# A graph layer on one core: moving the Q and V products of twelve node tiles out of the G stage, with x handed in transposed

## The chip, the cores and the metric

The kernel runs on one core of a Trainium2 chip. The metric is the device time of one execution in microseconds; lower is better. Three timed runs of the kernel before gave 1563.94, 1565.83 and 1568.54 us. The engines are called PE (TensorE, with PEld for its weight loads), DVE (VectorE), ACT (ScalarE), POOL (GpSimd) and SP (SyncE, here used only to start DMAs).

## The reference

One layer over N = 6250 nodes with D = 512 features and 106,250 directed edges (50,000 random ones in both directions, and one self loop per node), sorted by destination. All weights are 512 x 512.

```python
Q = relu(x @ Wq + bq);  V = x @ Wv + bv
# _former: attention without a softmax
Q = relu(layer_norm(Q));  H = sum(Q, axis=1)**2
H = pi / (2 * 2*(max(H) - min(H))) * H
cosQ, sinQ = Q * cos(H), Q * sin(H)
former = (cosQ @ (cosQ.T @ V) + sinQ @ (sinQ.T @ V)) / (cosQ @ sum(cosQ) + sinQ @ sum(sinQ) + 1e-10)
# _gcn: every node sums its neighbours' rows of G = x @ Wg
gcn = segment_sum((x @ Wg)[src] * dinv[src] * dinv[dst], dst) + bg     # dinv = 1/sqrt(degree)
out = relu(layer_norm(former + gcn + V) * gamma + beta)
return layer_norm(x + out)
```

## The kernel before

The nodes are cut into 49 tiles of 128 (the last has 106 rows); each matrix product with x is carried as three products of rounded parts (hi x hi, hi x lo, lo x hi), so one tile of x times one weight matrix is 12 matmuls of 128x512. There are two long parts.

**The G stage** (`g_tile`, tiles t = 0 to 48). SP loads a tile of x; PE turns it with four transposes (`g_turn`, L1363), ACT rounds the turned tile to its hi part (`g_step`, L601), DVE makes the lo part (`g_split`, L959), PE multiplies by Wg (12 matmuls, L1320 to L1322), ACT copies the result to SBUF (`g_keep`, L605). Beside it:
- For the first 31 tiles PE and DVE also count the node degrees: per tile three sets of one-hot rows (`bins`, L948 on DVE, 27 small matmuls L1376 on PE).
- ACT squares each tile of G (`square`, L610): 8 of them early, then from tile 31 on three per tile. From tile 35 on the gather table is written: ACT makes the hi half of a row pair (`pair_hi`, L616), DVE the lo half (`pair_split`, L865), SP stores it to DRAM (`table_store`, L403). Three or four pairs go with each tile (`pairs_until`), in a ring of 4 buffers: `pair_hi(n)` waits until pair n-4 has been stored. In five of these iterations DVE first works out scale factors (`factors`, L851 to L858) for the next group.
- For the first 37 tiles the hi and lo parts are stored to DRAM (`xt_store`), 512 KB a tile, to be loaded again later. For the last 12 tiles (`FUSED = 12`) PE makes Q and V at once from the parts that are there (`qv_beside_g`, 24 matmuls), and DVE and ACT carry them on.

Within one iteration of ACT the order is: round tile t+2, keep G of tile t, squares, `pair_hi`. Within one iteration of DVE it is: split tile t+2 (which waits for ACT's round), factors, then `pair_split` of the pairs that ACT made an iteration earlier. On SP it is: load of a coming tile, then the table stores.

**The run of 882 steps** (49 destination tiles with 18 steps each). Each step gathers the table rows of 128 edges: POOL issues an indirect DMA (L550), DVE makes a one-hot matrix (L1066), PE adds them up with two f16 matmuls (`chunk`, L1436 and L1438). The other work is laid between these chunks by tables of numbers: `qv_at(t)` starts Q and V of a tile every 6 steps (37 tiles, the first three before step 0), `cos_at` and `sin_at` run the two sweeps of moments (every 10/3 and every 3 steps a tile; 14 and 12 f16 matmuls each), `out_at` the output (every 7 steps a tile). Between the loops stand short serial parts (angles, moments). Every 18 steps the finished destination tile is combined with V and with the tile's own rows of G, which are loaded back from the table (`own_load`, `add_own`, two DVE instructions).

Of the kernel before, what the change touches and what calls it, by code (L numbers as in the profile page):

```python
# [6 lines left out]
F32 = mybir.dt.float32  # L7
# [31 lines left out]
def build_layer(nc, x, src, dst, Wq, bq, Wv, bv, Wg, bg, gamma, beta, out):  # L39
    N, D = x.shape  # L40
    E = src.shape[0]
# [16 lines left out]
    COLS = GROUPS * P  # L58
    LN_EPS = 1e-5
# [9 lines left out]
    COS_END = COS_AT + 10 * (TILES - 1) // 3 + 3  # L69
    SIN_AT = COS_END + 6  # L70
    SIN_END = SIN_AT + 3 * (TILES - 1) + 3
    OUT_AT = SIN_END + 6
    assert B == 4 and TAIL and FULL == 48 and SCALED < QV_TILES and OUT_AT + 7 * FULL < STEPS
# [7 lines left out]
    turned_x = nc.dram_tensor("turned_x", [TILES * P, 2 * D], F32).ap()  # L81

    ctx = ExitStack()
    with ctx:
# [16 lines left out]
        with nc.sbuf_tensor("operands_f16", [P, 8, 2 * D], F16) as operands_f16:  # L101
            pass
# [41 lines left out]
        edge_banks = banks[6], banks[7], banks[0], banks[6]  # L144
# [7 lines left out]
        dst_nat = part(0).bitcast(I32)  # L152
        src_nat = part(12).bitcast(I32)
        src_f = part(13)
# [20 lines left out]
        own_rows = pairs[:, 0, :]  # L175
# [48 lines left out]
        WIDE = 32  # L224

        def x_slot(t):
            return t % 2 if t < WIDE else t % 4

        def x_loads_until(t):
            return sum(x_slot(u) == x_slot(t) for u in range(t + 1))  # L230
# [5 lines left out]
        for name in (  # L236
            "setup_done", "pads_set", "dst_loaded", "src_loaded", "bias_loaded", "g_x_turned",
            "pair_hi", "pair_split", "factors_ready", "squared", "dst_placed", "own_added", "own_linked", "own_loaded", "combined_stored",
# [5 lines left out]
            "q_kept", "q_roomed", "q_hi", "q_paired", "late_roomed", "late_hi", "late_paired", "v_squared", "angle_ready", "cos_sin_ready", "m_summed", "m_hi", "moment_ready",  # L244
            "moment_hi", "sums_kept", "sums_turned", "cs_rounded", "o_products", "o_hi", "o_norm_ready", "o_stats1", "o_squared1", "o_squared2",
            "o_final", "o_scaled2", "dve_chain", "edges_f", "ident_ready", "raw_split",
            "edges_turned", "edges_kept", "limits_ready", "limits_turned", "ranges_ready",
# [10 lines left out]
        x_loaded = [sem(f"x_loaded{n}") for n in range(3)]  # L258
        xt_stored = [sem(f"xt_stored{n}") for n in range(4)]
# [28 lines left out]
        def nth(t):  # L288

            return (t + FUSED) % TILES  # L290

        def q_tile(t):

            return tile_of(nodes, nth(t))

        def qv_at(t):
            return 6 * (t - QV_RING)

        def cos_at(t):
            return COS_AT + 10 * t // 3  # L300

        def sin_at(t):
            return SIN_AT + 3 * t

        def out_at(n):
            return OUT_AT + 7 * n
# [5 lines left out]
        LAST_TILE = {4: 4, 7: 3, 9: 4, 10: 5, 12: 6, 13: 7, 15: 9, 16: 10, 17: 11}  # L312

        def late(t, at):

            return LAST_TILE[at] if t == QV_TILES - 1 else at

# [7 lines left out]
        def q_room(t):  # L325

            n = nth(t) % 2
            return stage[:, n, :] if t < QV_TILES else pairs[:, 1 + n, 0:D]

        def pair_at(n):  # L330

            return 8 + 12 * n

        def squares_room(t):
            return stage[:, 2, :] if t < QV_TILES else combine[:, 0:D]

        def v_slot(t):
            return t % QV_RING if t < QV_TILES else 1 + nth(t) % 2

        def v_stores_before(t):  # L340
            return t // QV_RING + (v_slot(t) > 0) * (FUSED // 2) if t < QV_TILES else nth(t) // 2

# [8 lines left out]
        def _(sp):  # L351

            whole, left = (GROUPS - 1) * P, E // P - (GROUPS - 1) * P

            def edge_views(nat):
                return nat.rearrange("p (g e) -> p g e", e=P)

            def full_groups(ap, nat, arrived):
                sp.dma_start(edge_views(nat)[:, 0:GROUPS - 1, :],
                             ap[0:whole * P].rearrange("(g p e) -> p g e", p=P, e=P)).then_inc(arrived, 16)  # L360

            def last_group(ap, nat, arrived):
                sp.dma_start(edge_views(nat)[0:left, GROUPS - 1, :],
                             ap[whole * P:(whole + left) * P].rearrange("(p e) -> p e", e=P)).then_inc(arrived, 16)
                sp.dma_start(edge_views(nat)[left:left + 1, GROUPS - 1, 0:E - E // P * P],
                             ap[E // P * P:E].rearrange("(p e) -> p e", p=1)).then_inc(arrived, 16)

            full_groups(dst, dst_nat, s["dst_loaded"])
            sp.wait_ge(s["pads_set"], 1)
            last_group(dst, dst_nat, s["dst_loaded"])  # L370
            def g_load(t):
                r, n = rows_of(t), x_slot(t)
                if t in (WIDE + 2, WIDE + 3):
                    sp.wait_ge(s["degrees_summed"], 1)
                else:
                    sp.wait_ge(s["g_x_turned"], freed(t, 2 if t < WIDE + 2 else 4))
# [33 lines left out]
            for t in range(0, TILES):  # L410
                if t <= WIDE:
                    g_load(t + 2)
# [1238 lines left out]
```

## Time and profile before

| | |
|---|---|
| runs | 1563.94, 1565.83, 1568.54 us; median 1565.83 |
| profiled execution, first to last instruction (span) | 1564.0 us |
| PE / PEld busy | 1493.1 us (95%) / 942.9 us (60%) |
| DVE / ACT / POOL busy | 1060.7 (68%) / 497.6 (32%) / 921.2 us (59%) |
| mean granted TensorE clock | 0.982 |
| G stage, up to the first chunk on PE | 313.7 us |
| from the first chunk to the end | 1250.3 us |

The span is the whole program on the device; what lies around it in a timed run is the 1.8 us to the median. A busy share is an average over stages, so the rows below go stage by stage. On PE a matmul is pipelined: the duration shown for a 128x512 matmul is 0.38 to 0.40 us, but the next one starts 0.21 to 0.24 us after it, and it is these distances between starts that add up to the time.

### The profile page before, as it was taken

What the parts mean: (1) busy time and instruction counts of PE and PEld (TensorE: products, weight loads), DVE (VectorE), ACT (ScalarE), POOL (GpSimd) and SP (SyncE); (2) the same over time, 40 slices, a digit from 0 to 9 for tenths busy, and PEclk for the clock granted to TensorE, in tenths of its full rate; (3) what the DMA queues carried; (4) which work ended last, traced back from release to release, by engine and by line L of the source; (5) the groups of instructions that cost most, each with busy time, mean ns of one, the idle gap of its engine ahead of it and who ended that gap; (6) DMA issues with size and microseconds to landing.
All of it is one profiled execution on the core that took longest, in us unless ns stands there. A gap on an engine that the chain in (4) does not pass through costs nothing.

```text
span 1564.0 us, 24480 instructions
## 1 busy us (share of the span) xinstructions
PE 1493.1 (95%) x7911; PEld 942.9 (60%) x7911; DVE 1060.7 (68%) x2945; ACT 497.6 (32%) x1010; POOL 921.2 (59%) x1022
## 2 busy tenths in 40 slices
PE   5999999899999997999998999989999999999995
PEld 3777788666666663444443444437777777767763
DVE  6999577677777676444445544457878877878785
ACT  2322776533333222111111111113333333333332
POOL 0000000277777775777776777777777777777772
PEclk9999999999999997999999999999999999999997
DMA  6555544699999998889888999889999999999894
GB/s 237 183 183 183 175 157 150 235 311 311 331 309 331 299 325 246 286 286 302 284 285 260 292 296 307 294 248 314 298 290 311 304 294 294 312 288 309 279 315 130
DMA packets 172753, 423.84 MB, mean 271 GB/s; under 512 B 24142, under 2 KB 25802, under 8 KB 172616
## 3 DMA queue, kind: packets, MB, share of 16 engines
q0 software_dynamic: 71120, 236.74, 48.1%
q1 hardware_dynamic: 79980, 146.16, 27.3%
q10 hardware_dynamic: 21516, 39.29, 6.6%
q8 instruction: 65, 1.06, 0.3%
q14 instruction: 72, 0.59, 0.1%
HBM read 351.42 MB, written 70.67 MB: 270 GB/s over the span
## 4 chain that ended last, share of the span: by engine, by line
PE 83%; DMA 6%; DVE 6%; issue 2%; ACT 2%; POOL 1%; SPq 0%; POOLq 0%; DVEq 0%; ACTq 0%
PE bank L1320 18%; PE bank L1321 17%; PE bank L1322 17%; PE bank L1436 12%; PE bank L1438 11%; DMA gathered<-scaled_g,index_slots 3%; DVE stage L948 2%; PE bank L1567 1%; PE bank L1376 1%; DMA stage<-in_x 1%; PE bank L1363 1%; POOL gathered L550 1%; DMA combine<-values 1%; PE bank L1504 1%; PE bank L1507 1%
## 5 line engine op out<-in xcount | busy, mean ns | idle before, releaser
L550 POOL DMA_INDIRECT gathered<-scaled_g,index_slots x882 | 882.9, 1001 | 305.7 <-issue 187.7
L1066 DVE TENSOR_SCALAR one_hot<-iota_bf,dst_in_tile,gathered 128x128 bf16<-128x128 bf16 x882 | 268.8, 326 | 327.4 <-DMA gathered<-scaled_g,index_slots 300.5
L1320 PE MATMUL bank<-weights,operands 128*128 128x512 f32 x784 | 395.5, 504 | 6.6 <-DVE stage L966 6.1
L1436 PE MATMUL bank<-gathered,one_hot 128*128 128x512 f16 x882 | 344.1, 390 | 25.7 <-DVE one_hot L1066 25.6
L1438 PE MATMUL bank<-gathered,one_hot 128*128 128x512 f16 x882 | 339.0, 384 | 0.0
L1321 PE MATMUL bank<-weights,operands 128*128 128x512 f32 x784 | 311.3, 397 | 0.0
L1322 PE MATMUL bank<-weights,operands 128*128 128x512 f32 x784 | 310.7, 396 | 0.0
L535 POOL COPY dst_slots<-dst_cols 128x18 f32 x49 | 13.9, 284 | 301.8 <-issue 299.6
L1320 PEld LDWEIGHTS bank<-weights,operands 128*128 128x128 f32 x784 | 149.1, 190 | 69.4 <-DVE stage L966 7.0
L1436 PEld LDWEIGHTS bank<-gathered,one_hot 128*128 128x128 bf16 x882 | 85.9, 97 | 171.1 <-issue 74.9
L707 ACT ACTIVATE operands_f<-operands,cos_sin_v 128x512 f16<-128x512 f32 x98 | 69.5, 720 | 335.8 <-PE bank L1322 201.6
L1322 PEld LDWEIGHTS bank<-weights,operands 128*128 128x128 f32 x784 | 148.1, 189 | 36.3
L1321 PEld LDWEIGHTS bank<-weights,operands 128*128 128x128 f32 x784 | 149.3, 190 | 22.6
L1322 PE MATMUL bank<-operands_f,nodes 128*128 128x512 f16 x392 | 148.5, 379 | 0.0
L1320 PE MATMUL bank<-operands_f,nodes 128*128 128x512 f16 x392 | 148.5, 379 | 0.0
L1321 PE MATMUL bank<-operands_f,nodes 128*128 128x512 f16 x392 | 148.5, 379 | 0.0
L724 ACT ACTIVATE operands<-stage,stats 128x512 fp32r<-128x512 f32 x98 | 70.9, 724 | 218.8 <-DVE stats L1203 218.8
L1438 PEld LDWEIGHTS bank<-gathered,one_hot 128*128 128x128 bf16 x882 | 87.9, 100 | 48.3 <-issue 3.6
L948 DVE TENSOR_TENSOR stage<-iota_bf,pairs 128x450 bf16<-128x450 bf16 (+1 forms) x186 | 95.6, 569 | 2.8 <-PE bank L1376 0.7
L1320 PE MATMUL bank<-gathered,operands 128*128 128x512 f32 (+1 forms) x196 | 84.8, 433 | 0.0
L1321 PE MATMUL bank<-gathered,operands 128*128 128x512 f32 (+1 forms) x196 | 78.5, 401 | 0.0
L1322 PE MATMUL bank<-gathered,operands 128*128 128x512 f32 (+1 forms) x196 | 78.2, 399 | 0.0
(231 smaller groups left out, 1916.3 us busy)
## 6 DMA issues: line engine op xcount, KB each, us to landing
operands<-values SPq DMA_DIRECT2D x98, 256.0 KB, 5.7
stage<-in_x SPq DMA_DIRECT2D x96, 256.0 KB, 3.8
turned_x<-operands SPq DMA_DIRECT2D x37, 512.0 KB, 3.1
operands<-turned_x SPq DMA_DIRECT2D x37, 512.0 KB, 6.4
gathered<-scaled_g,index_slots POOLq DMA_INDIRECT x882, 5.2
scaled_g<-pairs SPq DMA_DIRECT2D x49, 260.0 KB, 2.1
pairs<-scaled_g SPq DMA_DIRECT2D x49, 260.0 KB
values<-stage ACTq DMA_DIRECT2D x49, 256.0 KB, 4.8
```

What stands on the lines that cost most here:

```text
L550: pool.indirect_dma_start(out=plain(row_ring[k % RING]), out_offset=None, in_=table, in_offset=bass.IndirectOffsetOnAxis(ap=index_slots[:, ...
L707: act.activation(v_hi, m_values(g), ACT.Copy, scale=column(cos_sin_v, g % TILES * 2 + g // TILES))\
L724: act.activation(operands[:, 5 + n % 2, :], stage[:, 2 + j, :], ACT.Square, bias=st[:, 1:2], accum_out=st[:, 2:3]).then_inc(s[f"o_squared{ ...
L948: last = dve.tensor_tensor(hot[:, 0:count, :].rearrange("p c (j two) -> p c j two", two=2), iota_bf[:, 0:width].rearrange("p (j two) -> p ...
L1066: dve.tensor_scalar(one_hot[:, k % HOT, :], iota_bf[:, :], column(dst_in_tile, seq % 2 * PER_TILE + k), scale_of(row), ALU.is_equal, ALU.m ...
L1320: pe.matmul(out_ap, a_hi, b_hi, start=start and n == 0, stop=False, skip_group_check=True)
L1321: pe.matmul(out_ap, a_hi, b_lo, start=False, stop=False, skip_group_check=True)
L1322: last = pe.matmul(out_ap, a_lo, b_hi, start=False, stop=stop and n == len(pairs) - 1, skip_group_check=True)
L1363: last = pe.transpose(bank_[:, b * P:b * P + r], x_in[0:r, b * P:(b + 1) * P], ident[0:r, 0:r])
L1376: last = pe.matmul(banks[5][:, 0:TILES], mod_hot[half][:, c, :], div_hot[half][:, c, 0:TILES], start=False, stop=False, skip_group_check=True)
L1436: pe.matmul(gcn_banks[seq % 2][:, :], one_hot[:, k % HOT, :], hi, start=k == 0, stop=False, skip_group_check=True)
L1438: pe.matmul(gcn_banks[seq % 2][:, :], one_hot[:, k % HOT, :], lo, start=False, stop=False, skip_group_check=True).then_inc(s["chunk_summed ...
```

## The change

1. x is also handed in transposed by tiles and padded to 49 full tiles (`x_turned`), and the edge lists are handed in padded and in the layouts that the kernel used to make by transposing on PE. The transposes, `xt_store` and the loads of 512 KB go. ACT rounds and DVE splits straight from the loaded tile (`g_round`, `g_split`).
2. `FUSED` goes. The G stage makes G alone. All 49 tiles of Q and V are made in the run of steps; there x is loaded again (256 KB a tile) and split again by ACT and DVE (`x_round`, `x_split`).
3. The tables of numbers change: a tile of Q and V every 16/3 steps, of the sweeps every 20/7, of the output every 27/4. The number of steps stays at 882.
4. The own rows of G are added when V is made (`own_sum`, one DVE instruction, and a second store of 256 KB on ACT's queue), in place of `own_load` and `add_own`. The squares of V move from DVE to ACT (`v_square`).

The rules that pace the squares, the table's pairs and the factors (`squares_until`, `pairs_until`, `FACTOR_GROUPS`, `PAIRS = 4`) are the same.

```diff
-    FUSED = 12
-    QV_TILES = TILES - FUSED
-    HEAD, DRAIN = 6 * QV_RING, 24
-    LAST_QV = 6 * (QV_TILES - 1 - QV_RING)
+    HEAD, DRAIN = 18, 24
+    def qv_at(t):
+        return 16 * (t - QV_RING) // 3
+    LAST_QV = qv_at(TILES - 1)
     ANGLES = LAST_QV + 9
     COS_AT = ANGLES + 7
-            return COS_AT + 10 * t // 3
+        return COS_AT + 20 * t // 7
-            return SIN_AT + 3 * t
+        return SIN_AT + 20 * t // 7
-            return OUT_AT + 7 * n
+        return OUT_AT + 27 * n // 4
...
+            def g_load(t):
+                sp.wait_ge(s["g_summed"], freed(t, XT_RING))
+                sp.dma_start(operands_raw[:, 4 + t % XT_RING, :], x_turned[t, :, :])...
-            def xt_store(t): ...
+            def x_load(t):
+                if t < XT_RING:
+                    sp.wait_ge(s["g_summed"], done(TILES - XT_RING + t))
+                else:
+                    sp.wait_ge(s["q_summed"], freed(t, XT_RING))
+                sp.dma_start(operands_raw[:, 4 + qv_slot(t), :], x_turned[t, :, :])...
...
             for n in range(pairs_until(TILES - 1), TILES):
                 pair_hi(n)
-            for u in (TILES, TILES + 1, TILES + 2):
-                beside_g(u)
+            x_round(0)
...
+            x_split(0)
             for n in range(pairs_until(TILES - 1), TILES):
                 pair_split(n)
-            keep_beside_g(TILES)
...
+            def own_sum(t):
+                dve.scalar_tensor_tensor(own_room(t), q_tile(t), column(own_scale, t), v_room(t), ALU.mult, ALU.add)
-            def add_own(seq): ...
...
             def g_tile(t, n, r):
                 pe.wait_ge(s["g_x_split"], done(t))
-                if t + 2 < TILES:
-                    g_turn(t + 2)
                 pe.wait_ge(s["g_kept"], freed(t, 2))
                 ...
-                if t >= QV_TILES:
-                    qv_beside_g(t)
```

On ACT, in the last third of the G stage, an iteration stood like this before (round, keep, squares, pairs, then Q and V of an earlier tile):

```order
L601 CAST operands<-bank 128x512
L605 COPY nodes<-bank 128x512
L610 ACTIVATE squares_out,row_square<-nodes 128x512 x3
L616 ACTIVATE pairs<-nodes,row_factor 128x512 x3
L622 DMA values<-stage 128x512
L627 ACTIVATE nodes<-nodes 128x512
L632 ACTIVATE stats<-stats,small 128x1
L639 ACTIVATE nodes,row_sum<-nodes,stats 128x512
```

and stands like this now (`operands_raw` is the loaded tile of transposed x):

```order
L530 CAST operands<-operands_raw 128x512
L538 COPY nodes<-bank 128x512
L543 ACTIVATE squares_out,row_square<-nodes 128x512 x3
L549 ACTIVATE pairs<-nodes,row_factor 128x512 x3
L530 CAST operands<-operands_raw 128x512
```

The four rows of Q and V are gone; round, keep, three squares and the pairs are as they were.

On DVE, at the very end of the G stage, a last set of factors was followed by the last table pairs and then V, Q and the square of V of the last fused tile. Now the split of the first x tile for the steps (L877) stands between the factors and the last four pairs:

```order
L773 TENSOR_TENSOR row_factor<-row_factor,dinv 128x4
L877 TENSOR_TENSOR operands<-operands_raw,operands 128x512
L780 SCALAR_TENSOR_TENSOR pairs<-nodes,row_factor,pairs 128x512
L781 COPY pairs<-row_scale 128x1
L780 SCALAR_TENSOR_TENSOR pairs<-nodes,row_factor,pairs 128x512
L781 COPY pairs<-row_scale 128x1
```

So the last pairs wait behind an instruction that waits for ACT to have made all pairs' hi halves and rounded that tile.

On DVE, between the chunks of the Q and V loop, this piece stood before (L994 is the lo half of Q, L1008 the square of V, L966 and L971 add the biases to V and Q):

```order
L994 SCALAR_TENSOR_TENSOR nodes<-stage,nodes 128x512
L1008 SCALAR_TENSOR_TENSOR stage,row_v_square<-stage 128x512
L278 TENSOR_LOAD schedule
L278 ISA x2
L1066 TENSOR_SCALAR one_hot<-iota_bf,dst_in_tile,gathered 128x128 x2
L986 RECIPROCAL stats<-stats 128x1
L987 SCALAR_TENSOR_TENSOR stats<-stats 128x1
L971 TENSOR_TENSOR nodes<-bank,bias 128x512
```

and this one stands now (L877 splits the next x tile, L892 is the own row plus V, L961 the one-hot of a chunk):

```order
L898 TENSOR_TENSOR nodes<-bank,bias 128x512
L877 TENSOR_TENSOR operands<-operands_raw,operands 128x512
L961 TENSOR_SCALAR one_hot<-iota_bf,dst_in_tile,gathered 128x128
L912 RECIPROCAL stats<-stats 128x1
L913 SCALAR_TENSOR_TENSOR stats<-stats 128x1
L961 TENSOR_SCALAR one_hot<-iota_bf,dst_in_tile,gathered 128x128
L884 TENSOR_TENSOR stage<-bank,bias 128x512
L961 TENSOR_SCALAR one_hot<-iota_bf,dst_in_tile,gathered 128x128
L904 BN_STATS bn_parts<-nodes 128x6
L905 BN_AGGR stats<-bn_parts 128x2
L892 SCALAR_TENSOR_TENSOR pairs<-nodes,own_scale,stage 128x512
```

Per tile the square of V has left DVE, and the split and the own sum have come.

## Rows read from the trace of the kernel before

**Rows 1.** Page, part 1: busy time and share of each engine.
```profile
PE 1493.1 (95%) x7911; PEld 942.9 (60%) x7911; DVE 1060.7 (68%) x2945; ACT 497.6 (32%) x1010; POOL 921.2 (59%) x1022
```

**Rows 2.** Windows over step loops: us, PE, PEld, DVE, ACT, POOL busy, clock, DMA share, GB/s.
```profile
313.70:589.30 275.60, 274.55 (x1203) 175.11 (x1201) 199.08 (x551) 90.70 (x191) 205.18 (x223) 1.00 0.94 316
...
620.50:839.40 218.90, 218.56 (x1025) 99.51 (x1023) 98.42 (x246) 33.81 (x47) 166.25 (x184) 1.00 0.89 288
...
852.50:1046.20 193.70, 191.15 (x896) 85.89 (x895) 89.94 (x222) 31.82 (x45) 149.99 (x165) 1.00 0.90 292
...
1058.00:1531.30 473.30, 472.69 (x2591) 334.74 (x2590) 381.26 (x1219) 165.72 (x377) 350.93 (x386) 1.00 0.92 300
```

**Rows 3.** Same windows, chunk matmuls L1438 alone: PE busy and count.
```profile
313.70:589.30 275.60, 75.04 (x198) 19.73 (x198) 1.00 0.94 316
...
620.50:839.40 218.90, 61.77 (x163) 15.95 (x163) 1.00 0.89 288
```

**Rows 4.** Timeline of PE, two chunks in a row: start us, us, instruction.
```profile
319.55 0.39 PE L1436 MATMUL bank<-gathered,one_hot 128*128 128x512 f16 x1
...
319.99 0.38 PE L1436 MATMUL bank<-gathered,one_hot 128*128 128x512 f16 x1
```

**Rows 5.** Timeline, a tile of the degree-counting part: PE, then DVE.
```profile
90.47 0.63 PE L1363 MATMUL bank<-ident,stage 128*128 128x128 f32 x4
90.86 0.48 PE L1320 MATMUL bank<-gathered,operands 128*128 128x512 f32 x1
...
94.69 0.63 PE L1363 MATMUL bank<-ident,stage 128*128 128x128 f32 x4
...
146.64 0.69 DVE L959 TENSOR_TENSOR operands<-bank,operands 128x512 fp32r<-128x512 f32 x1
147.25 2.02 DVE L948 TENSOR_TENSOR stage<-iota_bf,pairs 128x450 bf16<-128x450 bf16 x4
149.19 1.08 DVE L905 TENSOR_TENSOR nodes<-nodes 128x896 f32<-128x896 f32 x1
```

**Rows 6.** Timeline of the start: ACT, DVE, PE.
```profile
11.42 1.90 ACT L586 CAST gathered<-nodes 128x2048 fp32r<-128x2048 f32 x1 [8.07 <-DMA nodes<-in_L_gnn_Wg]
...
13.35 2.29 DVE L822 TENSOR_TENSOR gathered<-nodes,gathered 128x2048 fp32r<-128x2048 f32 x1 [7.38 <-ACT gathered L586]
...
21.25 0.78 PE L1320 MATMUL bank<-gathered,operands 128*128 128x512 f32 x1
...
22.68 0.63 PE L1320 MATMUL bank<-gathered,operands 128*128 128x512 f32 x1
```

**Rows 7.** Timeline, table writing beside G: ACT, DVE, then PE with Q and V.
```profile
181.34 0.56 ACT L601 CAST operands<-bank 128x512 fp32r<-128x512 f32 x1
...
188.92 0.57 ACT L601 CAST operands<-bank 128x512 fp32r<-128x512 f32 x1
...
193.10 2.16 ACT L616 ACTIVATE pairs<-nodes,row_factor 128x512 f16<-128x512 f32 x3 [0.87 <-DMA scaled_g<-pairs]
195.16 0.56 ACT L601 CAST operands<-bank 128x512 fp32r<-128x512 f32 x1
...
190.13 0.74 DVE L865 SCALAR_TENSOR_TENSOR pairs<-nodes,row_factor,pairs 128x512 f16<-128x512 f32 x1
...
201.02 0.60 PE L1363 MATMUL bank<-ident,stage 128*128 128x128 f32 x4
...
209.85 0.60 PE L1363 MATMUL bank<-ident,stage 128*128 128x128 f32 x4
```

**Rows 8.** Windows in the G stage after the degrees.
```profile
160.00:180.00 20.00, 20.00 (x101) 16.41 (x100) 8.03 (x24) 16.84 (x43) 0.00 (x0) 1.00 0.68 224
180.00:200.00 20.00, 17.68 (x73) 13.59 (x72) 13.77 (x43) 16.07 (x35) 0.00 (x0) 0.91 0.38 134
```

**Rows 9.** Timeline of ACT at the end of the G stage.
```profile
276.47 0.56 ACT L605 COPY nodes<-bank 128x512 f32<-128x512 f32 x1
...
294.29 0.72 ACT L616 ACTIVATE pairs<-nodes,row_factor 128x512 f16<-128x512 f32 x1 [4.71 <-DMA scaled_g<-pairs]
```

More of the change, by code:

```diff
@@ L36, in freed, with build_layer @@
     return n + (1 + LEAD - depth)
[L39 removed]
+def build_layer(nc, x, x_turned, src_by_chunk, dst_by_chunk, dst_flat, edges, Wq, bq, Wv, bv, Wg, bg, gamma, beta, out):
     N, D = x.shape
[L41 removed]
+    E = edges
     B = D // P
@@ L101, in build_layer @@
         with nc.sbuf_tensor("operands_f16", [P, 8, 2 * D], F16) as operands_f16:
+            pass
+        with nc.sbuf_tensor("operands_raw", [P, 8, D], F32) as operands_raw:
             pass
@@ L222, in rows_of, with qv_slot @@
             return TAIL if t == FULL else P
[L224 to L230, printed above, removed]
+        def qv_slot(t):
+            return (TILES + t) % XT_RING
         def column(ap, c):
@@ L325, in q_room, with v_room, own_room @@
         def q_room(t):
[L327 to L341, printed above, removed]
+            return stage[:, t % 2, :]
+        def v_room(t):
+            return stage[:, 3 + t % QV_RING, :]
+        def own_room(t):
+            return pairs[:, t % QV_RING, 0:D]
         def in_flight(begin, tiles, q):
@@ L1250, in _ @@
                         combine_tile(seq - 1)
-                    if k == 16:
-                        add_own(seq)
                 if q == STEPS:
                     combine_tile(FULL)
-                for t, at in in_flight(qv_at, QV_TILES, q):
-                    if at == 4:
+                for t, at in in_flight(qv_at, TILES, q):
+                    if at == 2 and t + 1 < TILES:
+                        x_split(t + 1)
+                    if at == late(t, 4):
                         v_keep(t)
-                    if at == 5:
-                        v_square(t)
+                    if at == late(t, 5):
+                        own_sum(t)
                     if at == late(t, 7):
@@ L1457, in qv_step @@
             def qv_step(t, at):
-                j = t % QV_RING
+                j, slot = t % QV_RING, qv_slot(t)
                 if at == 0:
-                    pe.wait_ge(x_loaded[j], t // QV_RING * 16 + 16)
+                    pe.wait_ge(s["x_split"], done(t))
                     if t == 1:
@@ L1629, in _, with turned, padded_edges, by_chunk @@
                         end_tile(seq, surplus)
-_INS = ["x", "src", "dst", "L0_gnn_Wq", "L0_gnn_bq", "L0_gnn_Wv", "L0_gnn_bv", "L0_gnn_Wg", "L0_gnn_bg",
-        "L0_gnn_gamma", "L0_gnn_beta"]
+_INS = ["L0_gnn_Wq", "L0_gnn_bq", "L0_gnn_Wv", "L0_gnn_bv", "L0_gnn_Wg", "L0_gnn_bg", "L0_gnn_gamma", "L0_gnn_beta"]
+def turned(x):
+    n, d = x.shape
+    tiles = -(-n // P)
+    padded = np.zeros((tiles * P, d), x.dtype)
+    padded[:n] = x
+    return np.ascontiguousarray(padded.reshape(tiles, P, d // P, P).transpose(0, 3, 2, 1).reshape(tiles, P, d))
+def padded_edges(ends, fill):
+    padded = np.full(-(-ends.size // (P * P)) * P * P, fill, ends.dtype)
+    padded[:ends.size] = ends
+    return padded
+def by_chunk(flat):
+    return np.ascontiguousarray(flat.reshape(-1, P).T)
 def kernel(**inputs):
```

431 lines of the change are left out of this document (151 added, 280 removed).

## The prediction

> **What bounds the kernel now.** I read the page's busy shares first: PE is busy 95% of the span, no other engine over 68% [rows 1]. An average can hide a stage with another limit, so next come the windows over the loops of steps. In the loop of Q and V PE is busy 274.55 of 275.60 us, in the cosine sweep 218.56 of 218.90, in the sine sweep 191.15 of 193.70, in the output loop 472.69 of 473.30; DVE, ACT and POOL all have room there [rows 2]. So in the steps work added to PE is paid in full. Then the timeline of the G stage, in three pieces. While degrees are counted, a tile takes 4.22 us on PE (90.47 to 94.69) with no gap [rows 5]. Then come tiles 31 to 35, some 19 us, where ACT is busy 16.84 of 20 with the squares [rows 8]. From tile 35 on the table is written, and two periods are to be seen. Before Q and V join, ACT goes round in 188.92 to 195.16 = 6.24 us, and in an iteration with factors in 181.34 to 188.92 = 7.58 us; once they have joined, a tile takes 8.83 us on PE (201.02 to 209.85) [rows 7]. The question is which period is left when Q and V are taken out.
>
> **The steps.** I count from the first chunk (313.7) to the end, 1250.3 us, and take each loop by itself.
> - Q and V: 198 steps are 33 tiles [rows 3], so a tile costs 274.55/33 = 8.32 us of PE. Six of its chunks are in that; a chunk is 0.44 us (319.55 to 319.99) [rows 4], so the 24 products alone are 8.32 - 2.64 = 5.68 us. Now a tile has 16/3 chunks: 5.68 + 2.35 = 8.03 us. Steps 0 to 240 hold 45 tiles: 361.3 us against 275.6, **+85.7**.
> - Cosine sweep: 163 steps are 48.9 tiles [rows 3] with 14 + 6.67 f16 matmuls, 218.56/(48.9 x 20.67) = 0.216 us each [rows 2]. Now 14 + 5.71 = 19.71 a tile: 49 x 4.26 = 208.9, **-10.0**.
> - Sine sweep: 191.15/(49 x 18) = 0.217 us each [rows 2]; now 12 + 5.71: 49 x 3.84 = 188.1 against 193.7, **-5.6**. POOL, busy 149.99 of 193.70 there for 147 steps [rows 2], gets a little more time a step (1.34 us instead of 1.32).
> - Output: a quarter of a chunk less a tile, 48 x 0.25 x 0.44 = **-5.3**.
> - The serial parts between the loops stay as they are: 0.
> Sum +64.8 us. It is nearly the 12 moved tiles, 12 x 5.68 = 68.2; the new spacing only hands the 882 chunks round. The edits beside PE I cost at nothing. DVE has 199.08/33 = 6.0 us of work in a tile of 8.3 now [rows 2]; it loses the square of V (one 128x512 pass, like the 0.6 us that L959 holds DVE from 146.64 to 147.25 [rows 5]) and `add_own` (two passes per 18 steps), and gains the split and the own sum (two passes a tile): again about 6.0 of 8.0. ACT, 90.70/33 = 2.7 us a tile, gains a round and a square: about 4.0 of 8.0. DMA moves less (256 KB in place of 512 KB of x, one more store, one load less). If that cover failed, the price is the first rival's on the slow side.
>
> **The start of the G stage.** The first product stood at 21.25, behind the rounding of Wg (ACT 11.42 to 13.3), its split (DVE 13.35 to 15.6), the copies of edge columns and the transposes [rows 6]. Now the edges need no PE and are done before Wg has landed; after 15.6 only one split of 0.6 us is left, so the first product comes at 16.2: **-5.1**. Bounds: 0 if Wg lands 5 us later among the four x loads that are now issued early, -6 at best.
>
> **Degrees, tiles 0 to 30.** The transposes go: 94.69 - 90.86 = 3.83 us a tile is left of 4.22 [rows 5], 0.39 x 31 = 12. DVE is the next limit: two one-hot sets take 147.25 to 149.19, so 0.97 each, three of them and a split 3.5 us [rows 5]; in the eight tiles that also split a piece of Wq or Wv it is 4.1, and in the three with an edge reduction of 1.08 us it is 4.6, where nothing is won. I take **-10**; bounds -5 (DVE and PE wait for each other through the two buffers) and -13.
>
> **Tiles 31 to 35**: ACT's work does not change; 0.
>
> **Tiles 36 to 46, table writing.** Without Q and V the matmuls need only 12 x 5.68/24 = 2.8 us a tile, and what is left is a ring over three engines. ACT rounds a tile (188.92); DVE splits it and only then the pairs (the first at 190.13); SP stores them and ACT may fill the buffer again at 193.10; three pairs later, at 195.16, it goes round [rows 7]. The change removes nothing of this: the order on ACT and DVE is the same but for Q and V. So 11 x 6.24 + 5 x 1.3 for the factors = 75 us, against 181.34 to 276.47 = 95.1 now [rows 7, 9]: **-20**. The bounds are 57 us (ACT's own work alone: 5.9 us in the six iterations with three squares, 4.3 in the other five) and 84 (each store landing 0.8 us later on the mean; one wait near the end was 4.71 in place of 0.87 [rows 7, 9]).
>
> **Tiles 47 and 48, and the last pairs.** From 276.47 to the end of the last `pair_hi` at 295.0 it was 18.5 us, 4.71 of it waiting for a store that stood in SP's queue behind three loads of 512 KB [rows 9]. These are 256 KB now and sooner: about 11 us, **-7.5** (bounds -3 and -10). Then the first chunk came 18.7 us later, at 313.7. Now three Q and V tiles, 17 us, start 1.2 us after `pair_hi`, at the low clock at first, 2 us more; and the last four pairs are split behind `x_split(0)`, so that gathers start about 2 us later than they did after `pair_hi`. Both give about 20: **+1.5** (0 to +5).
>
> Sum of the G stage: -5.1 - 10 - 20 - 7.5 + 1.5 = -41. With +64.8 the span goes from 1564.0 to 1587.8. The runs' median is 1.8 above the span, so **1589 us**. In one sentence: PE gives up 12 x 5.68 = 68 us in a place where another ring leaves it idle afterwards, and takes them on where it is full.
>
> **A rule weighed.** What the trace shows is this: the 128x512 product is 0.63 us long at the start, and 1.43 us for three at the start, 0.48 each, stand against 0.237 (5.68/24) in the steps [rows 6, 2], and where PE idled 2.3 of 20 us the granted clock was 0.91 in place of 1.00 [rows 8]. A G tile at the low level would take 12 x 0.48 = 5.7 us, still under 6.24, but over the 3.8 that a tile takes ACT in tiles 31 to 35 (19/5). The Trainium skill (TensorE: Matmul & The Clock Gate, HAM oscillation) says that idle gaps of PE between bursts bring the clock down to half, each time anew. By that rule the table stretch would run at 1.2 GHz at no cost, and the sum stays 1589; if it reached back to tile 31 it is the third rival.
>
> **The rivals.**
> 1. *The table is not the limit, the stage falls to the matmuls.* The ring closes only because ACT, DVE and SP wait for each other; if it ran at ACT's own work (57 us in place of 75) the time is 1571, and if the stage went at PE's 2.8 us a tile it would be 11 x 3.4 = 38 us shorter still than 75: 1551, faster than before. For it: in before PE was never seen waiting for the table. Against it: 6.24 stands in the trace before any Q and V, and ACT's squares and pairs alone are 5.9 us. It decides from the point where the iteration drops below about 4.2 us. Chance 0.05 for 1571, 0.05 for 1551.
> 2. *The loop of Q and V is no longer paced by PE.* DVE and ACT each have one more hand-over a tile (round, split, own sum). If a tile took 8.5 us in place of 8.03, 45 of them are +21: 1610. For it: DVE is at three quarters and works in order. Against: in the output loop DVE is busy 381.26 of 473.30 and PE still 99.9% [rows 2]. Chance 0.12.
> 3. *The low clock reaches tiles 31 to 35.* PE would idle 0.4 of 3.2 us there; five tiles at 5.7 us in place of 3.8 are +9.5: 1598. Against: gaps of that size occur in the degree part without a loss. Chance 0.08.
> 4. *The added products hide behind gathers.* Then the steps would grow by less than 41 us and the kernel be faster, at about 1550. It needs PE idle in the steps, and rows 2 show 1157 of 1161.5 us busy. Chance 0.03.
> The forecast has 0.67.
>
> **How the numbers follow.** Range: forecast 1589 with its terms' bounds added as independent ones, about +-12; stretched down to the 1571 case and up towards the 1610 case: 1570 to 1607. A measurement of this kernel tells 0.3% from no change, 4.7 us. Faster than 1561: rivals 1 (its second half) and 4 without their overlap, 0.08. Within 0.3%, up to 1570.5: 0.06, from the low tail of the forecast and half of 1571. Slower: 0.86.
>
> **What would show it.** In the new profile the first chunk should stand near 272 us. PE should be idle about half of the time in the stretch before it, with ACT waiting for stores of the table and an ACT period of 6.2 us; the degree tiles should take 3.8 to 4.1 us each. The Q and V loop should hold 240 steps in 361 us with PE full, and the sweeps take 209 and 188 us. The forecast is wrong if PE shows gaps in the steps (then rival 2), or if the table stretch shows less than 5 us a tile (then rival 1).

## The result

| | before | after |
|---|---|---|
| median of the runs | 1567.18 us (1563.94 to 1568.56, 4 runs) | 1583.92 us (1581.33 to 1584.23, 4 runs) |
| ratio to before | | 1.0109, 95% interval 1.0094 to 1.0124 |
| span of the profiled execution | 1564.0 us | 1582.3 us |

The changed kernel is 1.1% slower. 1589 us was forecast, with 1570 to 1607 as the range. The spans differ by 18.3 us where the terms had given +23.8.

The page's first part answers to [rows 1]. PE is as full as before, and ACT has gained:

```profile
PE 1479.6 (94%) x7701; PEld 924.0 (58%) x7701; DVE 1025.0 (65%) x2842; ACT 554.2 (35%) x1145; POOL 913.2 (58%) x1020
```

The windows over the four loops of steps (steps 0 to 240, 256 to 396, 402 to 542, 548 to 872) answer to [rows 2], with the same columns (us, busy time of PE, PEld, DVE, ACT, POOL, granted clock, DMA share, GB/s):

```profile
276.58:637.28 360.70, 360.70 (x1577) 233.07 (x1576) 259.01 (x676) 161.70 (x360) 247.77 (x271) 1.00 0.91 294
665.55:874.43 208.88, 208.55 (x977) 95.03 (x976) 82.03 (x200) 33.92 (x47) 146.41 (x158) 1.00 0.84 260
887.64:1074.78 187.14, 187.14 (x882) 85.12 (x880) 80.12 (x199) 32.61 (x46) 141.44 (x158) 1.00 0.88 282
1086.40:1557.29 470.89, 470.89 (x2587) 335.40 (x2586) 351.57 (x1167) 165.27 (x377) 334.40 (x375) 1.00 0.89 285
```

The last window of [rows 2] ends 4.3 us ahead of step 872. Over the same steps (536 to 872 there) the output loop before was 477.6 us long:

```profile
1058.06:1535.65 477.59, 476.98 (x2613) 337.58 (x2611) 381.64 (x1220) 166.31 (x377) 354.24 (x390) 1.00 0.92 299
```

The loop of Q and V runs from the first chunk at 276.58 to step 240 and lasts 360.7 us with PE full (before: 275.6). The two sweeps and the output loop are 10.0, 6.6 and 6.7 us shorter. The G stage ends 37.2 us earlier (313.79 to 276.58). That is what the change buys with 85 us.

Windows from the end of the degrees to the end of table writing, to be read against [rows 8]:

```profile
140.00:160.00 20.00, 18.76 (x103) 14.20 (x102) 10.53 (x25) 13.02 (x31) 0.00 (x0) 1.00 0.27 79
160.00:180.00 20.00, 13.90 (x52) 10.08 (x50) 10.43 (x33) 16.80 (x38) 0.00 (x0) 0.83 0.39 133
180.00:200.00 20.00, 13.42 (x36) 9.93 (x36) 10.99 (x34) 15.67 (x34) 0.00 (x0) 0.74 0.48 169
200.00:220.00 20.00, 11.50 (x43) 8.54 (x42) 10.88 (x33) 13.74 (x28) 0.00 (x0) 0.74 0.43 154
220.00:240.00 20.00, 12.81 (x37) 9.12 (x36) 11.01 (x37) 12.78 (x23) 0.00 (x0) 0.74 0.39 143
```

From 160 us on no engine is full. PE is shown busy 11.5 to 13.9 of 20, DVE 11, ACT 13 to 17, and the DMA engines 0.39 to 0.48. Where no engine is full the engines wait for each other, and the question is whether the waits close to a ring. Those in 165 to 245 us (us in total, times, longest) name its links:

```profile
DVE operands L871 <- ACT operands L530: 35.0, 11, 4.3
ACT pairs L549 <- DMA scaled_g<-pairs: 21.0, 13, 3.2
...
PE bank L1201 <- DVE operands L871: 15.3, 7, 3.2
```

ACT waits for DMA here and nowhere for PE: no such line is in the list. So neither PE's products nor its low clock hold ACT up.

One turn of the ring, in the timelines of ACT, DVE and SP, answers to [rows 7]:

```profile
174.13 0.60 ACT L530 CAST operands<-operands_raw 128x512 fp32r<-128x512 f32 x1
...
178.31 2.21 ACT L549 ACTIVATE pairs<-nodes,row_factor 128x512 f16<-128x512 f32 x3 [0.84 <-DMA scaled_g<-pairs]
180.43 0.60 ACT L530 CAST operands<-operands_raw 128x512 fp32r<-128x512 f32 x1
...
174.76 0.69 DVE L871 TENSOR_TENSOR operands<-operands_raw,operands 128x512 fp32r<-128x512 f32 x1 [3.01 <-ACT operands L530]
175.37 0.75 DVE L780 SCALAR_TENSOR_TENSOR pairs<-nodes,row_factor,pairs 128x512 f16<-128x512 f32 x1
...
176.21 2.49 SPq L358 DMA_DIRECT2D scaled_g<-pairs  x4
```

ACT rounds a tile at 174.13. DVE had waited 3.01 us for that, splits at 174.76 and only then makes the pair (175.37). SP stores it at 176.21, it lands, ACT fills the freed buffer at 178.31 and three pairs later rounds again at 180.43. The turn is 6.30 us. Before, the same turn stood at 6.24.

Behind the last product of G PE has nothing to do for 15.1 us. Its first product of Q or V waits for the split of that tile on DVE, which waits for ACT's round, and on ACT that round stands behind all the pairs:

```profile
255.76 0.79 PE L1201 MATMUL bank<-weights,operands 128*128 128x512 f32 x1 [15.06 <-DVE operands L877]
```

Until the first chunk only the products of three tiles of Q and V follow (255.76 to 276.35). No run rounds that tile earlier, so what this wait costs is open.

### The profile page after: what moved, and what is told of

Its sections match the earlier page's. It is cut to its first block, busy times and chain, and to the rows that moved or that the text cites. A ratio compares the mean times of both kernels' runs of the same rounds, so it can differ in the third digit from the quotient of the medians.

```text
span 1582.3 us, 24082 instructions
## 1 busy us (share of the span) xinstructions
PE 1479.6 (94%) x7701; PEld 924.0 (58%) x7701; DVE 1025.0 (65%) x2842; ACT 554.2 (35%) x1145; POOL 913.2 (58%) x1020
## 4 chain that ended last, share of the span: by engine, by line
PE 85%; DVE 8%; ACT 3%; DMA 3%; issue 1%; SPq 0%; DVEq 0%; ACTq 0%
PE bank L1201 19%; PE bank L1202 18%; PE bank L1203 18%; PE bank L1277 13%; PE bank L1279 12%; DVE stage L862 3%; DMA scaled_g<-pairs 2%; PE bank L1407 1%; DVE operands L871 1%; ACT pairs L549 1%; ACT squares_out L543 1%; DVE pairs L780 1%; PE bank L1234 1%; PE bank L1395 1%; PE bank L1394 1%
## 5 line engine op out<-in xcount | busy, mean ns | idle before, releaser
L961 DVE TENSOR_SCALAR one_hot<-iota_bf,dst_in_tile,gathered 128x128 bf16<-128x128 bf16 x882 | 270.9, 325 | 232.3 <-DMA gathered<-scaled_g,index_slots 187.3
L1201 PE MATMUL bank<-weights,operands 128*128 128x512 f32 x784 | 406.4, 518 | 15.1 <-DVE operands L877 15.1
L1277 PEld LDWEIGHTS bank<-gathered,one_hot 128*128 128x128 bf16 x882 | 85.7, 97 | 164.9 <-issue 76.6
L473 POOL COPY dst_slots<-dst_cols 128x18 f32 x49 | 12.7, 259 | 250.9 <-issue 247.3
L1201 PE MATMUL bank<-gathered,operands 128*128 128x512 f32 x196 | 90.0, 459 | 16.4 <-DVE operands L871 16.2
L1039 DVE SCALAR_TENSOR_TENSOR operands_f<-operands,cos_sin_v,operands_f 128x512 f16<-128x512 f32 x98 | 73.4, 749 | 38.1 <-ACT operands_f L631 38.0
L1202 PE MATMUL bank<-gathered,operands 128*128 128x512 f32 x196 | 83.0, 423 | 0.0
```

Source lines behind the costliest of these rows:

```text
L961: dve.tensor_scalar(one_hot[:, k % HOT, :], iota_bf[:, :], column(dst_in_tile, seq % 2 * PER_TILE + k), scale_of(row), ALU.is_equal, ALU.m ...
L1039: dve.scalar_tensor_tensor(v_lo, m_values(g), column(cos_sin_v, g % TILES * 2 + g // TILES), v_hi, ALU.mult, ALU.subtract).then_inc(s["m_s ...
L1201: pe.matmul(out_ap, a_hi, b_hi, start=start and n == 0, stop=False, skip_group_check=True)
L1202: pe.matmul(out_ap, a_hi, b_lo, start=False, stop=False, skip_group_check=True)
L1277: pe.matmul(gcn_banks[seq % 2][:, :], one_hot[:, k % HOT, :], hi, start=k == 0, stop=False, skip_group_check=True)
```

## The experiments

The first chunk's time is that of its second matmul, as above. "Kept" is ACT's copy of a tile out of its bank (L538). Unless another kernel is named, an edit is made to the changed kernel.

**e1: the pairs ahead of the split on DVE.** The ring's link from ACT's round over the split to the pairs is cut.

```diff
             for t in range(0, TILES):
+                for n in range(pairs_until(t - 2), pairs_until(t - 1)):
+                    pair_split(n)
                 g_split(t + 2)
                 ...
-                for n in range(pairs_until(t - 2), pairs_until(t - 1)):
-                    pair_split(n)
```

> The changed kernel, but on DVE the table pairs of the last iteration are split before the coming x tile is, not after it. Theory (the table ring ACT round, DVE split of x, DVE split of pairs, store, ACT again sets the last part of the G stage): the ring opens, the period of tiles 36 to 46 falls from about 7.0 us (77.4 us for eleven) to ACT's own work, about 5.9 us with three squares and 4.3 us with one, in all some 57 to 62 us. Time about 1584 - 18 = 1566 us (1562 to 1572). Rival (ACT's work or the matmuls themselves set that part): no change, 1582 to 1586 us.

Measured: 1560.12 us, ratio to before 0.9971 (0.9958 to 0.9984); the first chunk at 251.71, 24.9 us earlier than in the changed kernel. The loops of steps are the same to 0.1 us. Windows of the same stretch:

```profile
160.00:180.00 20.00, 14.63 (x56) 10.72 (x55) 14.01 (x46) 19.18 (x45) 0.00 (x0) 0.91 0.55 186
180.00:200.00 20.00, 12.66 (x46) 9.07 (x45) 14.29 (x46) 19.42 (x43) 0.00 (x0) 0.85 0.61 209
200.00:220.00 20.00, 16.91 (x63) 12.62 (x62) 17.46 (x55) 19.75 (x40) 0.00 (x0) 0.90 0.68 247
```

ACT is now busy 19.2 to 19.8 of 20: the ring has gone and an engine's own work is the limit. From the keep of tile 36 (166.98) to that of tile 47 (219.74) it is 52.8 us, against 76.9 in the changed kernel and 57 to 62 expected; the time lies under the expected range of 1562 to 1572 us too. This swap of two lines on DVE gives back more than the whole change had lost.

**e2: 31 squares early instead of 8.** Takes ACT's work out of the stretch and leaves the ring.

```diff
-        EARLY_SQUARES = 8
+        EARLY_SQUARES = 31
```

> The changed kernel, but ACT squares every tile of G as it comes during the degree tiles (31 early squares in place of 8), so it has two squares fewer in each iteration from tile 31 to 41. Ring theory: tiles 31 to 35 fall from 19 us to PE's 14.5, tiles 36 to 46 stay at about 77 us because the store and the splits are waited for, not ACT: 1584 - 5 = 1579 us. Rival (ACT's work sets the last part): also six iterations by 1.6 us each, 1569 us or less.

Measured: 1586.47 us, ratio 1.0141 (1.0124 to 1.0158); first chunk 278.55. The ring theory's size missed, 1579 being expected. Its core held: tiles 36 to 47 take 76.9 us from keep to keep as before (168.69 to 245.59), with fewer squares on ACT, so ACT's work is not what sets them (45.5 us of it in these tiles against 54.3). Tiles 31 to 36 took 15.0 us instead of 19.6. But 6.2 us were lost where nothing was expected: tile 31 is kept at 153.67 instead of 147.44, because a degree tile takes 4.12 us instead of 3.82 (each the mean of the 16 tiles from keep 11 to keep 27, as for e4 and e11). ACT and DVE in such a tile:

```profile
103.45 0.59 ACT L538 COPY nodes<-bank 128x512 f32<-128x512 f32 x1 [2.29 <-PE bank L1203]
104.07 0.63 ACT L543 ACTIVATE squares_out<-nodes 128x512 bf16<-128x512 f32 x1
104.70 0.60 ACT L530 CAST operands<-operands_raw 128x512 fp32r<-128x512 f32 x1
...
105.34 0.69 DVE L871 TENSOR_TENSOR operands<-operands_raw,operands 128x512 fp32r<-128x512 f32 x1 [0.54 <-ACT operands L530]
105.94 3.00 DVE L862 TENSOR_TENSOR stage<-iota_bf,pairs 128x450 bf16<-128x450 bf16 x6
```

The square stands between the keep and the next round, and DVE, full in this part, waits 0.54 us for the round. e11 tests that reading.

**e3: both edits.**

> The changed kernel with both: pairs split first, and all squares early. Ring theory: tiles 31 to 35 at PE's pace, and tiles 36 to 46 at ACT's 4.3 us or, if PE is at its low clock there, at its 5.1 to 5.7 us: 47 to 62 us in place of 77. Time 1584 - 5 - 22 = about 1557 us (1550 to 1564), so faster than the kernel before. Rival (matmuls or DMA set that part): not under 1575 us.

Measured: 1557.63 us, ratio 0.9961 (0.995 to 0.9973); first chunk 250.05; tiles 36 to 47 in 49.9 us. The time is as expected. Of the 7.9 us of work that ACT has less in these tiles than in e1 (43.5 against 51.4), 2.9 are seen: no engine is full any more (PE 37.6, DVE 41.5 of 49.9), and ACT again waits 6.0 us for stores to land.

**e4: four transposes of 128x128 a tile put back on PE.** They compute nothing that is used; DVE and ACT do not wait for them. It asks what the removed transposes had cost.

```diff
             def g_tile(t, n, r):
                 pe.wait_ge(s["g_x_split"], done(t))
+                for b in range(B):
+                    pe.transpose(banks[1 + n][:, b * P:(b + 1) * P], ident[:, :], ident[:, :])
```

> The changed kernel with four PE transposes a tile put back into the G stage (of a constant, their result is not used). Theory: PE sets the degree tiles, so they are paid there, 31 x 0.39 = 12 us less what the DVE-bound tiles hide, and cost nothing in the tail, where PE waits: 1584 + 10 = 1594 us (1590 to 1597), first chunk 10 us later. Rivals: PE pays for them in all 49 tiles, +19 us, 1603; or DVE had set the degree tiles, +0 to +3.

Measured: 1590.24 us, ratio 1.0165 (1.0147 to 1.0183); first chunk 283.21. Tile 31 is kept at 154.87, 7.4 us later, and a degree tile takes 4.08 us instead of 3.82; table writing stays at 76.9. So +6.6 us in all. The direction is right and the size nearly 4 us smaller than expected: of the 0.39 us of PE a tile, 0.27 are seen. In the degree tiles DVE and PE are both nearly full (63.42 and 64.38 of 65 us in the changed kernel), so taking one's work away soon shows the other's.

**e5: two more passes of DVE in each tile of the Q and V loop**, into a room nobody reads.

```diff
+                for n in range(2):
+                    dve.scalar_tensor_tensor(<unused half of pairs[:, 3]>, q_tile(t), column(own_scale, t), v_room(t), ...)
                 dve.scalar_tensor_tensor(own_room(t), q_tile(t), column(own_scale, t), v_room(t), ALU.mult, ALU.add)
```

> The changed kernel with two more DVE instructions of 128x512 a tile in the Q and V loop (the own sum made twice more into unused memory). Theory (that loop is paced by PE, DVE has about 2 of 8.03 us free): DVE goes to about 7.3 of 8.03 us a tile, the loop stays at 361 us, time 1584 to 1588. Rival (DVE's hand-overs are near the limit): a tile goes to 8.5 us or more, the loop to 383 us, 1605 or more.

Measured: 1583.86 us, ratio 1.0123 (1.0106 to 1.014), no change against the changed kernel. The window of its Q and V loop:

```profile
276.58:637.30 360.72, 360.68 (x1576) 233.12 (x1577) 316.75 (x768) 161.60 (x362) 271.89 (x272) 1.00 0.92 294
```

DVE has 57.7 us more to do and PE does not notice. The loop is PE's, and costing the new DVE work at nothing was right.

**e6: the turned x and edges, without the moved Q and V.** The kernel before with x and the edges handed in transposed; the 12 fused tiles and the old spacing of the steps stay.

```diff
-            def g_step(t, n, r): ... # transposed on PE, rounded from the bank
-            def xt_store(t): ...
+            def g_round(t):
+                act.copy(operands[:, t % XT_RING, :], operands_raw[:, 4 + t % XT_RING, :])...
+            def g_load(t):
+                if t - XT_RING >= QV_TILES:
+                    sp.wait_ge(s["q_summed"], done(nth(t - XT_RING)))
...
             for t in range(0, TILES):
-                ... g_load(t + 2), g_load(t + 3) or g_load(t + 4), then xt_store(t)
+                g_load(t + XT_RING)
                 for n in range(pairs_until(t - 2), pairs_until(t - 1)):
                     table_store(n)
```

> The kernel before with only the first part of the change: x and the edges handed in transposed and laid out, no transposes, no stored parts, x loaded and split again in the steps; the twelve tiles of Q and V stay in the G stage, the step spacing, the own rows and the squares of V stay as before. Theory (moving the twelve tiles is what cost the time): start -4, degree tiles -10, twelve fused tiles -0.39 each -5, end of the G stage +-2, steps 0 to -3: 1566 - 19 = about 1547 us (1542 to 1553). Rival (handing x in and splitting it twice costs the time): not under 1566 us.

Measured: 1565.11 us (1558.94 to 1570.11), ratio 1.0002 (0.9984 to 1.0021), a miss by 18 us. The degrees did give their share (tile 31 kept at 148.41 instead of 162.33), and the fused tiles took it back: 8.3 to 12.4 us each instead of 8.7 to 9.4, first chunk at 312.43. SP's timeline there:

```profile
205.93 0.33 SPq L349 DMA_DIRECT2D operands_raw<-in_x_turned  x1
206.31 1.46 SPq L369 DMA_DIRECT2D scaled_g<-pairs  x3
```

The load of a coming tile stands ahead of the stores in both kernels. In the kernel before it waits for the transposes only and leaves long before the next stores:

```profile
193.50 0.45 SPq L377 DMA_DIRECT2D stage<-in_x  x1
198.39 1.77 SPq L403 DMA_DIRECT2D scaled_g<-pairs  x3
```

Here it overwrites the parts that PE still reads, and in a fused tile it waits for PE's product of Q. The pair had been ready at 205.1. ACT could go on only at 209.66, 3.35 us after the store's issue; it had been 2.1 in the kernel before.

**e7: e6 with the edits of e1 and e2**, the pairs here ahead of V and Q as well.

> As the run before, with the pairs split before the x tile and all squares early. Theory: in the fused part PE already sets 8.4 us a tile, so the ring hides there and only tiles 31 to 36 gain: 5 us from the squares and 2 to 4 from the two iterations before Q and V join: about 1540 us (1536 to 1546). Rival (the ring costs in the fused part too): under 1535.

Measured: 1600.06 us, ratio 1.0235 (1.0217 to 1.0253), 60 us off; a fused tile takes 14.7 to 16.4 us. ACT, DVE, SP and PE in one of them:

```profile
225.67 2.11 ACT L568 ACTIVATE pairs<-nodes,row_factor 128x512 f16<-128x512 f32 x3 [10.45 <-DMA scaled_g<-pairs]
...
226.42 0.75 DVE L812 SCALAR_TENSOR_TENSOR pairs<-nodes,row_factor,pairs 128x512 f16<-128x512 f32 x1 [8.73 <-ACT pairs L568]
...
222.09 0.33 SPq L349 DMA_DIRECT2D operands_raw<-in_x_turned  x1
222.46 1.42 SPq L369 DMA_DIRECT2D scaled_g<-pairs  x3
...
221.66 0.40 PE L1276 MATMUL bank<-weights,operands 128*128 128x512 f32 x1
...
229.34 0.79 PE L1274 MATMUL bank<-weights,operands 128*128 128x512 f32 x1 [4.49 <-DVE stage L915]
```

Here the ring closes over four engines. SP's load waits for the last product of Q (221.66), and behind it wait the stores (222.46) of pairs that DVE had made from 210.87 on. ACT gets its buffer at 225.67 and DVE its pair at 226.42. Only behind the pairs does DVE empty the bank of V (L915), and for that PE waits 4.49 us. The two edits that had gained 26 us in one kernel (e3) cost 35 in the other, in which a later wait stood ahead on SP and one more duty behind on DVE. The two edits were not tried apart here.

**e8: e6 with the stores first on SP.**

```diff
             for t in range(0, TILES):
-                g_load(t + XT_RING)
                 for n in range(pairs_until(t - 2), pairs_until(t - 1)):
                     table_store(n)
+                g_load(t + XT_RING)
```

> The kernel of e6 (x and edges handed in transposed, 12 fused tiles kept) with one thing moved: on SP, in an iteration of the G stage, the stores of the table pairs are issued before the load of x for tile t + 4, and not after it. Theory, queue order: in e6 that load waits for the Q product of a fused tile and stands ahead of the stores; at 205.93 and 228.02 the stores leave 0.8 us or more after the pair was ready, and where they leave right behind the load the first one lands 3.35 us after its issue, against 2.11 in the kernel before. With the stores first about 1 to 1.3 us goes from each of the 12 fused iterations: they return to 8.5 to 9 us, the first chunk comes at 295 to 301 us and the whole takes 1549 us (1545 to 1556). Rival, the ring alone: the order on SP does not matter, the fused iterations are long because the pairs wait in a loop through ACT's round and DVE's split; first chunk 310 to 313, 1565 us.

Measured: 1555.44 us, ratio 0.994 (0.9923 to 0.9956); first chunk 299.54. The order on SP alone moved the first chunk by 12.9 us between the two profiled executions and the median by 9.7, of the 18 by which e6 had missed; the fused tiles are back at 8.1 to 10.0 us.

**e9: e8, and on DVE the pairs behind V and Q, ahead of the split.**

```diff
                 keep_beside_g(t)
+                for n in range(pairs_until(t - 2), pairs_until(t - 1)):
+                    pair_split(n)
                 g_split(t + 2)
```

> As e8, and on DVE the lo halves of the pairs are made behind V, Q and the square of V of the fused tile and ahead of the split of tile t + 2. Theory, ring: this takes ACT's round and DVE's split out of the loop of the ring of 4, so a fused iteration is set by PE's 36 matmuls of 0.237 us, 8.5 us, or by ACT's own work; against e8 another 0 to 6 us go, 1546 us (1540 to 1552). Rival: with the pairs ahead of the split, PE gets its operands later, and the iterations grow as in e7 (15 us each): 1590 us or more.

Measured: 1542.42 us (1541.27 to 1543.99), ratio 0.9853 (0.9836 to 0.9869); first chunk 289.55. The fused tiles take 8.40 us on most turns, which is PE's time. Windows in their middle:

```profile
200.00:220.00 20.00, 20.00 (x91) 15.85 (x90) 16.59 (x51) 14.66 (x33) 0.00 (x0) 1.00 0.54 192
220.00:240.00 20.00, 20.00 (x88) 16.07 (x87) 14.72 (x45) 14.21 (x31) 0.00 (x0) 1.00 0.47 172
```

PE is full at the full clock while the table is written. This and e12 are the fastest versions, some 41 us under the changed kernel and 23 under the one before.

**e10: e3 with the stores first on SP.**

> The kernel of e3 (after, pairs first, squares early) with the stores ahead of the load on SP. In e3 the load of x mostly had nothing to wait for, but at 200.15 it held back stores whose first pair was ready at 198.5, and ACT waited 1.86 us for one of them. Theory, queue order: 1 to 4 us go, 1555 us (1552 to 1558). Rival: the stores now wait for their pairs in front of loads, tile x comes later, nothing or a loss of up to 3 us: 1557 to 1561.

Measured: 1556.34 us, ratio 0.9935 (0.9921 to 0.9949); first chunk 248.29, 1.8 us earlier than in e3. The two were not timed side by side and the ranges of their runs overlap (1554.1 to 1558.36 here), so a gain of 1 to 2 us is likely and not shown.

**e11: e3 with the early square behind the next round.** ACT waits there for PE anyway.

```diff
             for t in range(0, TILES):
                 g_round(t + 2)
+                if 1 <= t <= HIST_TILES:
+                    for n in range(squares_until(t - 2), squares_until(t - 1)):
+                        square(n)
                 ...
                 g_keep(t, t % 2)
-                for n in range(squares_until(t - 1), squares_until(t)):
-                    square(n)
+                if t >= HIST_TILES: ... # as before
```

> The kernel of e3 (after, pairs first, squares early), but ACT makes the square of an early tile behind the rounding of the next x tile, where it otherwise waits 2.3 to 2.9 us for PE, and not ahead of it. Theory: in e2 the early square delayed ACT's round, DVE's split waited 0.54 us for it in every degree tile (5.7 us over 11 waits in 65 to 130 us), and that made a degree tile 4.14 us instead of 3.85; behind the round the degree tiles return to 3.85, tile 31 is kept at 147 to 149 us instead of 153.7, and e3's 1557.6 becomes 1552 us (1549 to 1555). Rival: the longer degree tile comes from the mere presence of ACT's squares (memory or bank traffic), not from the order; degree tiles stay at 4.1 and the time at 1557.

Measured: 1550.46 us (1550.07 to 1551.72), ratio 0.9901 (0.9885 to 0.9918); first chunk 243.42. ACT and DVE in a degree tile:

```profile
102.89 0.59 ACT L538 COPY nodes<-bank 128x512 f32<-128x512 f32 x1 [2.02 <-PE bank L1207]
103.37 0.62 ACT L530 CAST operands<-operands_raw 128x512 fp32r<-128x512 f32 x1
103.90 0.63 ACT L543 ACTIVATE squares_out<-nodes 128x512 bf16<-128x512 f32 x1
...
104.06 0.68 DVE L873 TENSOR_TENSOR operands<-operands_raw,operands 128x512 fp32r<-128x512 f32 x1
```

DVE's split no longer waits, a degree tile takes 3.82 us as in the changed kernel (16 of them from 68.37 to 129.43), tile 31 is kept at 146.28. So the 6 us of e2 were the order of two instructions on ACT, and not the squares.

**e12: e9 with the squares of e11.**

> The kernel of e9 (x and edges turned, 12 fused tiles kept, stores first, pairs behind V and Q and ahead of the split) with the squares of 31 tiles made early, behind the rounding. In e9 tiles 31 to 36 take 25 us where ACT makes three squares and pairs in each; with the squares done they need one square each, and PE's products are 12 x 0.237 = 2.8 us. Theory: 5 to 8 us go there, nothing in the fused tiles, which PE's matmuls fill (8.40 us each): 1536 us (1532 to 1541). Rival: the squares are not what holds tiles 31 to 36, the pairs are: 1542 us.

Measured: 1543.79 us, ratio 0.9856 (0.9837 to 0.9876); no difference from e9, where 1536 was expected. Tiles 31 to 36 did take 15.0 us instead of 19.6, but the first chunk moved only from 289.55 to 288.95. The expectation's rival (the pairs hold these tiles) is false too. The keeps had been late there, PE had hardly: it begins the first fused Q and V at 166.31 in e9 and at 164.12 in e12. Through the fused tiles it is full in both, so e12 keeps a lead of 2.2 us to the keep of tile 48 (260.22 and 258.03), and 1.6 of it are gone at the first chunk; why was not tried.

## Why the prediction was right

By its own steps, from the two traces:

| step | predicted | measured |
|---|---|---|
| Q and V loop | +85.7 | +85.1 (360.7) |
| cosine / sine / output | -10.0 / -5.6 / -5.3 | -10.0 / -6.6 / -6.7 |
| serial parts between the loops and the end | 0 | -6.3 |
| first product | 16.2, -5.1 | 17.18, -4.1 |
| degrees | -10 | -10.7 |
| tiles 31 to 35 | 0 | 0 |
| tiles 36 to 46 | 75, -20 | 77.4, -17.7 |
| tiles 47, 48 and the last pairs | -7.5 | -8.1 |
| from there to the first chunk | +1.5 | +3.4 |
| span | +23.8 | +18.3 |

- **The loop of Q and V.** The sum 5.68 us for 24 products and 0.44 for each chunk gave 361.3 and it is 360.7. e5 shows that the cover over DVE's new work was real, with 57.7 us to spare at least. Rival 2 (8.5 us a tile) is false.
- **The ring.** This was the step that decided the sign, and e1 shows it by taking it away: without the link through the split it is 52.8 us from keep 36 to keep 47 in place of 76.9, with no work removed. e2 shows the other side: with work removed and the ring left, 76.9. The price of rival 1's first half (57 us, 1571) was near what e1 gave for that stretch (52.8, an ACT that works without a gap); it needed an edit that the change does not hold. In the changed kernel itself rival 1 is false. The term's second part, 5 x 1.3 us "for the factors", has a cause partly wrong. The turn of 7.58 us before had factors and a fourth pair too; in the changed kernel the turns from ACT's rounds at 194.27 and 209.17 take 7.35 and 7.00 us with four pairs and no factors, the one at 201.62 takes 7.55 with three pairs and factors. The 6.3 us stand only where there are three pairs and no factors, in four of the eleven turns. With seven longer turns in place of five the stretch came out 2.4 us over the forecast.
- **The degrees.** -10.7 with one size too large behind it: e4 puts 0.27 us a tile on the transposes and not 0.39, and only 7.4 of the 10.7 us return with them. The rest is not settled; the loads, the rounding and the split changed their sources too, and that was not tried apart.
- **The low clock.** It came where it had been placed: 0.74 to 0.83 from 160 us on, 1.00 in 140 to 160, so rival 3 is false. The rule of the Trainium skill (TensorE: Matmul & The Clock Gate, HAM oscillation) agrees with these windows in that the clock falls anew between bursts. It did not stay at 1.2 GHz, which would be 0.50, but went to and fro between the two levels. e3 writes the table in 49.9 us and is still at 0.83 and 0.91 in 180 to 220. That the low clock costs nothing in the table stretch of the changed kernel rests on its list of waits, where ACT never waits for PE; a run with the clock up was not made.
- **Added products behind gathers** (rival 4) is false by PE's 360.70 of 360.70 us.
- **What was missed.** The serial parts were put at 0 without a reason and gave 6.3 us: 2.9 from step 240 to 256 (198 to 214 before), 3.1 from step 872 to 881, 0.3 in the rest. The span came out 5.5 us under the sum, and the other steps nearly cancel: the sweeps and the output gave 2.4 more than expected, the Q and V loop 0.6, and the G stage 3.8 less. In e6 to e9 and e12, which have the old spacing, these two pieces take 30.4 to 32.0 and 11.4 to 12.7 us, against 28 and 8.5 to 10 in the other runs; so they go with the moved spacing or with the own sum. Which of the two was not tried. The term of the output loop was counted in chunks, so the window in [rows 2] that ends 4.3 us early did not touch it.

e9 says what the change was worth in its parts. The turned x and edges gain nothing with the load ahead of the stores (e6), 10 us with the stores first (e8, 1555.44 against 1565.43), and 23 with the pairs moved on DVE as well (e9); the move on DVE was not tried on the kernel before by itself. Taking the twelve tiles out of the G stage (with the new spacing, the own sum and the squares of V on ACT, which no run takes apart) is what loses. By the count the products that stood in the shadow of the table's writing are 12 x 5.68 = 68 us where PE is full, and they give back only what the ring leaves. How much is lost hangs on the ring: the changed kernel is 19 us slower than e6, but with the ring opened in both it is 8 us (e11 against e9, 1550.46 against 1542.42, the ratios 0.9901 and 0.9853 clear of each other), and e11 still has 10.0 us of PE's wait ahead of its first Q and V, where e9 has 3.9; e9 also has the stores first.

## What to carry to other kernels

Work taken off the fullest engine pays only until the next limit. Here, with no engine full, that limit was a ring: walk such a ring link by link in the timeline and price one turn before counting instructions. In this kernel swapping two pieces of work on one in-order engine moved the first chunk by 24.9 us (e1), 12.9 (e8) and 6.6 (e11), and each such swap holds only for the waits around it (e7). A stretch in which PE would idle is the place for its products, not a place to empty.

## What the runs showed of the hardware

- In e7 the level of the clock can be read off single rows. After 4.49 us without work PE's products stand 0.43 us apart (229.93, 230.36, 230.78), with a granted clock of 0.50 in 229.3 to 231.5; before that pause they stood 0.23 apart (221.66, 221.89), at 1.00 in 221.5 to 224.5. That is 1.2 against 2.4 GHz.

```profile
221.89 0.39 PE L1274 MATMUL bank<-gathered,operands 128*128 128x512 f32 x1
...
229.93 0.63 PE L1275 MATMUL bank<-weights,operands 128*128 128x512 f32 x1
230.36 0.63 PE L1276 MATMUL bank<-weights,operands 128*128 128x512 f32 x1
230.78 0.63 PE L1274 MATMUL bank<-weights,operands 128*128 128x512 f32 x1
```

- A table store of 260 KB frees its buffer 2.1 us after its issue where nothing was issued just ahead of it, and 3.35 us where a load of 256 KB was issued 0.38 us before it (e6 at 206.31; 3.21 us in e7 at 222.46).
